# Layer norms of a transformer block moved from VectorE to ScalarE, with the routing and last scaling cut into short pieces and some TensorE pieces joined

## The reference, cut to what matters

```python
x = x + attention(layernorm(x))                  # 16 heads of 64, 4 key/value heads
x = x + cross_attention(layernorm(x), ctx, mask) # 16 heads of 16, 64 context rows per batch
z = layernorm(x)
# the feed-forward part, on every row z:
cluster = argmax(calibrate(z @ cluster_sigs.T))           # 8 clusters
tile    = argmax(calibrate(z @ sigs.T)[8 of the cluster]) # 8 tiles in each
comp    = tanh(gelu(z @ cw1 + cb1) @ cw2 + cb2)
mag     = relu(comp @ w1[tile] + b1[tile]) @ w2[tile] + b2[tile]
y       = z + mag * directions[tile] * output_scale
x = x + (y - mean(y)) / sqrt(var(y) + eps) * gamma + beta
```

## Time and profile before

| | us |
|---|---|
| three runs | 2066.41, 2067.19 (median), 2070.11 |
| the profiled execution, whole | 2067.07 |
| its span in the trace | 2065.3 |

### The profile page before, as it was taken

One profiled execution on the slowest core, in us unless ns is written; L12 is line 12 of the kernel. 1 busy time (PEld: TensorE's weight loads), 2 busy tenths in 40 slices (PEclk: granted clock), 3 DMA queues, 4 the chain that ended last, 5 costly groups with the idle time before them and its releaser, 6 DMA issues.

```text
span 2065.3 us, 27531 instructions
## 1 busy us (share of the span) xinstructions
PE 1855.6 (90%) x9556; PEld 912.9 (44%) x9556; DVE 1378.7 (67%) x2925; ACT 1135.1 (55%) x1507; POOL 979.1 (47%) x763
## 2 busy tenths in 40 slices
PE   3799999988999799998999988998899989998863
PEld 2444453443644344453554435444364434444342
DVE  4466756667576776756578585766657676677656
ACT  1367755655466554655456554665546654575422
POOL 2065545634554444652645345563465535463621
PEclk7799999999999999998999999999899999999895
DMA  4020000000200000010200000010010000000000
GB/s 150 1 62 1 1 1 1 12 21 1 62 11 1 1 21 1 1 32 0 62 11 1 1 0 21 1 32 0 11 41 1 1 0 21 1 1 1 21 0 10
DMA packets 22875, 32.01 MB, mean 15 GB/s; under 512 B 2577, under 2 KB 16977, under 8 KB 22737
## 3 DMA queue, kind: packets, MB, share of 16 engines
q1 hardware_dynamic: 22736, 30.26, 5.3%
HBM read 13.48 MB, written 4.19 MB: 9 GB/s over the span
## 4 chain that ended last, share of the span: by engine, by line
PE 70%; DVE 18%; issue 5%; ACT 4%; POOL 2%; DMA 0%; SPq 0%; POOLq 0%; DVEq 0%; ACTq 0%
PE attended L955 19%; PE key_scores L935 18%; PE misc L853 7%; PE misc L995 5%; PE max_scores L903 5%; DVE relu L1432 3%; PE misc L1019 3%; PE misc L965 2%; PE misc L921 2%; PE misc L1051 1%; PE misc L1010 1%; PE misc L1040 1%; PE misc L858 1%; DVE prob_sum L1446 1%; DVE buf_b L1328 1%
## 5 line engine op out<-in xcount | busy, mean ns | idle before, releaser
L1189 ACT ACTIVATE probs<-key_scores 128x1024 f32<-128x1024 f32 x512 | 524.5, 1024 | 602.1 <-PE key_scores L935 420.6
L1792 POOL TENSOR_TENSOR prob_sum<-prob_sum,probs 128x512 f32<-128x512 f32 x384 | 538.9, 1403 | 234.0 <-ACT probs L1189 212.8
L955 PE MATMUL attended<-probs,v_all 128*64 128x512 f32 x2048 | 577.1, 637 | 0.1
L1432 DVE CUSTOM_DVE_ANT_0 relu<-max_scores,relu 128x512 f32<-128x512 f32 x512 | 332.3, 686 | 263.7 <-PE max_scores L903 262.6
L935 PE MATMUL key_scores<-q_high,k_chain 64*128 64x512 f32 x2048 | 470.2, 455 | 10.7 <-ACT probs L1189 10.3
L935 PEld LDWEIGHTS key_scores<-q_high,k_chain 64*128 64x128 f32 x2048 | 197.4, 189 | 468.3 <-issue 251.5
L1446 DVE TENSOR_TENSOR prob_sum<-prob_sum,probs 128x512 f32<-128x512 f32 x384 | 375.6, 978 | 19.6 <-ACT probs L1189 8.9
L1173 ACT ACTIVATE relu<-max_scores 128x1024 f32<-128x1024 f32 x256 | 261.5, 1021 | 47.2 <-PE max_scores L903 47.2
L903 PE MATMUL max_scores<-k_max,q_high 64*128 64x512 f32 x1024 | 215.5, 416 | 75.4 <-DVE row_max L1432 73.9
L1788 POOL TENSOR_TENSOR prob_sum<-probs 128x512 f32<-128x512 f32 x64 | 87.8, 1371 | 345.6 <-PE misc L965 286.6
L935 PE MATMUL key_scores<-q_low,k_chain 64*128 64x512 f32 x1024 | 207.8, 402 | 0.0
(11 more groups left out here) (406 smaller groups left out, 2170.5 us busy)
## 6 DMA issues: line engine op xcount, KB each, us to landing
k_chain<-k_chain SPq DMA_DIRECT2D x32, 256.0 KB, 3.8
buf_a<-in_x SPq DMA_DIRECT2D x8, 512.0 KB, 4.9
k_max<-k_max SPq DMA_DIRECT2D x16, 256.0 KB, 3.7
x_in<-in_x SPq DMA_DIRECT2D x7, 512.0 KB, 4.2
out_x<-buf_b SPq DMA_DIRECT2D x7, 512.0 KB, 3.0
heads_out<-in_qkv_wT SPq DMA_DIRECT2D x1, 1536.0 KB, 8.5
wo<-in_o_wT SPq DMA_DIRECT2D x1, 1024.0 KB, 12.7
rows_sb<-in_rows SPq DMA_DIRECT2D x1, 646.0 KB, 10.4
```

What stands on the lines that cost most here:

```text
L955: tensor.matmul(attended[head * HD:(head + 1) * HD, :], v_all[:, kt, g * HD:(g + 1) * HD], prob_slot(u, kt, head), start=kt == 0, stop=kt ...
L1189: scalar.activation(probs[(u * KT + kt) % len(probs)][:, :, :], key_scores[:, :, :], ACT.Exp).then_inc(S["exp"])
L1432: vector.tensor_tensor_reduce(out=relu[:, head, :], in0=max_scores[:, head, :], in1=relu[:, head, :], scale=1.0, scalar=-3.4e38, op0=ALU.a ...
L1792: gpsimd.tensor_tensor(prob_sum[1][:, :], prob_sum[1][:, :], probabilities, ALU.add).then_inc(S["prob_sum1"])
```

## The change

It does the following:

- **Norms on ACT.** `x_norm` and `norm` leave DVE. ACT computes x * rstd + (-mean * rstd) with an Identity activation of 128x256 for each of the four tiles, scale and bias being columns of `rstd`. For that `rstd` on POOL has four instructions in place of two (add eps, -mean, power, product), each waiting for the one before.
- **Statistics behind the additions.** `bn_stats` follows each `x1`, `x2` and `y` directly (and each pair of tiles of x in the new piece `x_bn`); `stats` keeps only `bn_aggr`.
- **Short pieces.** `cal_b` and `cal_c` (6 and 7 instructions) become `cal_b` to `cal_f` (3, 3, 2, 2, 3) with a `yield LATE` between them; `first_max`, `pick_tiles` and `pick_one` get steps of their own; `spline` becomes `spline_a` and `spline_b` (4 and 4); `y`, `gamma`, `beta` go by pairs of tiles. No DVE instruction of these changes.
- **Joined pieces.** Both transposes of a norm stand in one step, so do both parts of `q2`, `route` with `compress`, and the `gathered` matmuls by two; `stats` moves to the step of the last `x1`, and an empty step behind the second norm is dropped.
- New waits protect the reused buffers (`ahead_of`: all signals that the plan gave before this entry).

The core of the diff (the cuts inside `cal_b` to `cal_f`, `spline_a` and `spline_b`, and the loops by pair in `y`, `gamma_` and `beta_` are as told above):

```diff
-    "x_stats": {"bn_stats": NT, "moments": NT, "var_eps": 1, "rstd": 1}, "x_norm": {"normed": NT},
+    "x_bn": {"bn_stats": 2}, "x_stats": {"moments": NT, "var_eps": 2, "rstd": 2}, "x_norm": {"normed": NT},
...
-    "out_proj": {"out_proj": 1}, "residual_bias": {"residual_bias": 1}, "x1": {"x1": 1},
-    "stats": {"bn_stats": NT_TIMES, "moments": NT_TIMES, "var_eps": 1, "rstd": 1}, "norm": {"normed": NT_TIMES},
+    "out_proj": {"out_proj": 1}, "residual_bias": {"residual_bias": 1}, "x1": {"x1": 1, "bn_stats": 1},
+    "stats": {"moments": NT_TIMES, "var_eps": 2, "rstd": 2}, "norm": {"normed": NT_TIMES},
...
+        self.so_far[entry] = dict(self.total)
...
 def x_prep(plan, t):
     yield LATE
+    plan.put("x_bn", t, 0)
+    yield LATE
+    plan.put("x_bn", t, 1)
     plan.put("x_stats", t)
     yield LATE
     plan.put("x_norm", t)
...
-    plan.put("cal_b", j, which)
-    yield LATE
-    plan.put("cal_c", j, which)
+    for part in "bcdef":
+        plan.put(f"cal_{part}", j, which)
+        if part != "f":
+            yield LATE
...
-        yield EARLY if i < nt - 1 else LATE
+        if i < nt - 1:
+            yield EARLY
     plan.put("stats", j, 1)
     yield LATE
     plan.put("norm", j, 1)
     yield EARLY
     for c in range(KC):
         plan.put_in_bank("norm_T", j, 1, c)
-        yield LATE
+    yield LATE
+    for c in range(KC):
         if c < nt // 2:
             plan.put("output_bias", j, c)
         plan.put("norm_ev", j, 1, c)
-        yield EARLY
+    yield EARLY
...
     for m in range(KC):
         plan.put_in_bank("q2", j, m)
-        yield LATE
+    yield LATE
+    for m in range(KC):
         plan.put("q2_ev", j, m)
-        yield EARLY
+    yield EARLY
...
     plan.put("norm", j, 2)
-    yield LATE
     yield EARLY
     for c in range(KC):
         plan.put_in_bank("norm_T", j, 2, c)
-        yield LATE
+    yield LATE
+    for c in range(KC):
         plan.put("norm_ev", j, 2, c)
-        yield EARLY
+    yield EARLY
     plan.put_in_bank("route", j)
+    plan.put_in_bank("compress", j)
     yield LATE
     plan.put("route_ev", j)
-    yield EARLY
-    plan.put_in_bank("compress", j)
-    yield LATE
     plan.put("gelu", j)
...
     plan.put("tanh_b", j)
     yield from clusters
+    yield LATE
     plan.put("first_max", j, 0)
+    yield LATE
     plan.put("pick_tiles", j)
-    yield LATE
     yield from calibration(plan, j, 1)
+    yield LATE
     plan.put("first_max", j, 1)
+    yield LATE
     plan.put("pick_one", j)
-    yield LATE
     yield EARLY
     plan.put_in_bank("pickT", j)
     yield LATE
     plan.put("pickT_ev", j)
     yield EARLY
-    for i in range(nt):
-        plan.put_in_bank("gathered", j, i)
+    for pair in range(nt // 2):
+        for i in range(2 * pair, 2 * pair + 2):
+            plan.put_in_bank("gathered", j, i)
         yield LATE
-        plan.put("gathered_ev", j, i)
-        yield EARLY if i < nt - 1 else LATE
-    plan.put("spline", j)
-    plan.put("y", j)
-    yield LATE
+        for i in range(2 * pair, 2 * pair + 2):
+            plan.put("gathered_ev", j, i)
+        if pair < nt // 2 - 1:
+            yield EARLY
+    yield LATE
+    plan.put("spline_a", j)
+    yield LATE
+    plan.put("spline_b", j)
+    for pair in range(nt // 2):
+        yield LATE
+        plan.put("y", j, pair)
     plan.put("stats", j, 3)
-    yield LATE
-    plan.put("gamma", j)
-    yield LATE
-    plan.put("beta", j)
     for pair in range(nt // 2):
+        yield LATE
+        plan.put("gamma", j, pair)
+    for pair in range(nt // 2):
+        yield LATE
+        plan.put("beta", j, pair)
         plan.put("x3", j, pair)
-        if pair < nt // 2 - 1:
-            yield LATE
     plan.put("store", j)
...
+        def ahead_of(signal, stage, *key):
+
+            return S[signal], plan.so_far[(stage, *key)].get(signal, 0)
...
+            def normalise(space, src, dst):
+                for i in range(space.nt):
+                    scalar.activation(dst[:, i, :], src[:, i, :], ACT.Identity, bias=space.rstd[:, 3, i:i + 1],
+                                      scale=space.rstd[:, 1, i:i + 1]).then_inc(S["normed"])
+
+            def x_norm(t):
+                act.wait_ge(*after("rstd", "x_stats", t))
+                normalise(main, x_of(t), x_of(t))
+
+            def norm(j, k):
+                act.wait_ge(*after("rstd", "stats", j, k))
+                if k == 1 and j:
+                    act.wait_ge(*after("store", "store", min(j, FIRST_HALF) - 1))
+                if k == 1 and j == 0:
+                    act.wait_ge(*after("v2", "v2", B - 1))
+                    act.wait_ge(*after("v2_block", "v2_block", B - 1))
+                    act.wait_ge(*after("mask_add", "mask"))
+                if k == 2:
+                    act.wait_ge(*after("norm_T", "norm_T", j, 1, KC - 1))
+                normalise(spaces[j], spaces[j].a, spaces[j].b)
...
-            def measure(space, src, stage, *key):
-                nt, base = space.nt, before("bn_stats", stage, *key)
-                for i in range(nt):
+            def bn_stats(space, src, tiles):
+                for i in tiles:
                     vector.bn_stats(space.stats[:, i, :], src[:, i, :]).then_inc(S["bn_stats"])
-                for i in range(nt):
-                    dve.wait_ge(S["bn_stats"], base + i + 1)
+
+            def moments(space, stage, *key):
+                dve.wait_ge(*ahead_of("rstd", stage, *key))
+                for i in range(space.nt):
                     vector.bn_aggr(space.moments[:, i, :], space.stats[:, i, :]).then_inc(S["moments"])
 
-            def normalise(space, src, dst):
-                for i in range(space.nt):
-                    vector.tensor_scalar(dst[:, i, :], src[:, i, :], space.moments[:, i, 0:1], space.rstd[:, 1, i:i + 1],
-                                         ALU.subtract, ALU.mult).then_inc(S["normed"])
+            def x_bn(t, pair):
+                dve.wait_ge(*x_loaded(t))
+                dve.wait_ge(*ahead_of("moments", "x_bn", t, pair))
+                bn_stats(main, x_of(t), range(2 * pair, 2 * pair + 2))
 
             def x_stats(t):
-                dve.wait_ge(*x_loaded(t))
-                dve.wait_ge(S["normed"], plan.counts.get(("normed", "x_norm", t), (0, 0))[0])
-                measure(main, x_of(t), "x_stats", t)
-
-            def x_norm(t):
-                dve.wait_ge(*after("rstd", "x_stats", t))
-                normalise(main, x_of(t), x_of(t))
+                dve.wait_ge(*after("bn_stats", "x_bn", t, 1))
+                moments(main, "x_stats", t)
...
+                dve.wait_ge(*after("x1", "x1", j, i))
+                dve.wait_ge(*ahead_of("moments", "x1", j, i))
+                bn_stats(spaces[j], buf_a, [i])
 
             def stats(j, k):
-                if k == 1:
-                    dve.wait_ge(*after("x1", "x1", j, tiles_of(j) - 1))
-                elif k == 2:
-                    dve.wait_ge(*after("x2", "x2", j, tiles_of(j) // 2 - 1))
-                else:
-                    dve.wait_ge(*after("y", "y", j))
-                measure(spaces[j], spaces[j].b if k == 3 else spaces[j].a, "stats", j, k)
-
-            def norm(j, k):
-                dve.wait_ge(*after("rstd", "stats", j, k))
-                if k == 1 and j:
-                    dve.wait_ge(*after("store", "store", min(j, FIRST_HALF) - 1))
-                normalise(spaces[j], spaces[j].a, spaces[j].b)
+                dve.wait_ge(*ahead_of("bn_stats", "stats", j, k))
+                dve.wait_ge(*ahead_of("gamma", "stats", j, k))
+                moments(spaces[j], "stats", j, k)
...
+                dve.wait_ge(*after("x2", "x2", j, pair))
+                dve.wait_ge(*ahead_of("moments", "x2", j, pair))
+                bn_stats(spaces[j], spaces[j].a, range(2 * pair, 2 * pair + 2))
...
             def rstd(space, stage, *key):
+                epsilons, roots = before("var_eps", stage, *key), before("rstd", stage, *key)
                 pool.wait_ge(*after("moments", stage, *key))
+                pool.wait_ge(*ahead_of("normed", stage, *key))
+                pool.wait_ge(*ahead_of("beta", stage, *key))
                 gpsimd.tensor_scalar(space.rstd[:, 0, :], space.moments[:, :, 1], EPS, None, ALU.add).then_inc(S["var_eps"])
+                pool.wait_ge(S["var_eps"], epsilons + 1)
+                gpsimd.tensor_scalar(space.rstd[:, 2, :], space.moments[:, :, 0], -1.0, None, ALU.mult).then_inc(S["var_eps"])
                 pool.wait_ge(*after("minus_half", "minus_half"))
-                pool.wait_ge(*after("var_eps", stage, *key))
+                pool.wait_ge(S["var_eps"], epsilons + 2)
                 gpsimd.tensor_tensor(space.rstd[:, 1, :], space.rstd[:, 0, :], minus_half[:, 0:space.nt],
                                      ALU.pow).then_inc(S["rstd"])
+                pool.wait_ge(S["rstd"], roots + 1)
+                gpsimd.tensor_tensor(space.rstd[:, 3, :], space.rstd[:, 2, :], space.rstd[:, 1, :],
```

(4 more changed lines are left out.)

124 lines of the change are left out of this document (72 added, 52 removed), and 2 rows, old and new, of the table SIGNALS.

## The result

The changed kernel took **2076.27 us** (median of 6 runs, 2073.76 to 2084.20), the kernel before in the same series 2068.89 (2066.41 to 2070.26). The ratio is **1.0044, 95% interval 1.0024 to 1.0063**: slower by 0.4%, where 1960 was forecast and 1920 to 2015 given as the range.

A forecast was written before the change was run, and what follows sets the result against it. PE was taken as the bound, losing 116 us idle and 60 to a slow clock. Idle -73, clock -40, prologue +3 and last tails +3 gave -107 from 2067.07: 1960 us, range 1920 to 2015.

The forecast's parts named there:

- What bounds the kernel: Main loop: PE is the bound, with 116 us idle and 60 us of slow clock, 176 us at most to win.
- room: Tails: each step leaves DVE 0.88 us free; steps times this, against routing and scaling work, with 3 us of lag allowed.
- Routing and scaling in short pieces: Main-loop tails: waits for row maxima and last routing instruction fall from 64.6 + 8.3 to 15 us, bounds 5 and 40.
- Statistics behind the additions: DVE: same instructions, 1.65 us for four, spread over steps where DVE waited for PE; cost 0.
- Joined pieces: Tails: no matmul or evacuation removed, two ACT evacuations in one step; cost 0, bounds 0 and 0.5 us each.
- Norms off DVE: Norms moved to ACT: 0.45 to 0.5 us each, 2.0 for four; 14 us of waits left, from 21.9 and some of 10.3.
- the slower rival: Main loop's 20 norms: ACT waits for POOL's rstd and holds exponentials and scores; 2091 us, chance 0.05.
- Clock: Main loop: PE's loss to the slow clock falls from 60 to 20 us as gaps shrink, -40.
- The ends: Prologue and last tails, outside the main loop: each forecast 3 us longer.
- prologue: Before the attention: chunk 1's x_T comes about 4 us later; +3 us, 0 to +5.
- Last tails: Serial chain at the end: about four statistics each 0.6 us later, plus ACT norms; +3 us, -3 to +6.
- DVE stays the bound: Rival, main loop: instructions in twice the steps are still late, each also waiting for POOL's sums; 2012 us, chance 0.14.

The follow-up runs named there:

- v_ends_pool1: v_ends with POOL's running sum of head 1 cut to one column from the third key tile on, that softmax left out: 1950.73 us.
- v_joins: The kernel before with statistics moved and pieces joined (with x_prep's extra step), norms on DVE, no cuts: 2106.68 us.
- v_ends_dve: v_ends with the layer norms back on DVE, cuts and joins kept: 2075.10 us.
- v_sum_all: v_ends with POOL's running sums of head 1 moved to DVE, whole output computed: 2011.45 us.
- v_ends: The changed kernel with old pieces in the last two half tails and x statistics in one piece for the first two batches: 2077.29 us.
- v_nocut: v_ends with routing and last scaling in the old long pieces, joins and ACT norms kept: 2097.11 us.
- v_norms: The kernel before with norms on ACT and statistics behind the additions, no cuts or joins: 2076.22 us.
- v_stats: The kernel before with only the statistics moved behind the additions: 2082.74 us.
- v_best: v_sum_all with the norms of the last chunk's two halves on DVE again: 2010.13 us.

## Why the prediction was wrong

**What bounds the kernel** was read rightly: 176 us of idling and slow clock, mostly behind DVE pieces. In v_ends_pool1 the idle time of the attention is 41 us, where the forecast had 43. That is no hit of its sum: those 41 were reached with POOL's sums taken away, which by itself brings the kernel before from 116 to 72.

**The step that failed is "room"**: steps times 0.88 us of DVE time, against work counted at the durations of the old places. That room was taken from a unit without a tail, where no short SBUF instruction stands beside POOL's sums; and the durations are no property of the instruction. What DVE spends in the attention above the shortest duration of each kind of instruction grew from 273 to 313 us, though 39 of the 273 had been the norms': some 79 us of new waiting, 65 of it in the tail's instructions on the tiles of routing and scaling (40 to 105) and 13 in the attention's own sums. (The expectations' 257 and 287 take somewhat longer durations as the quiet ones.) The forecast had seen the effect for the norm (1.05 against 0.48) and used it for the part that leaves DVE, not for the 40 instructions that were to be spread over twice the steps. The 15 us of row maxima and last routing waits were 66.0 (57.6 + 8.4).

**Routing and scaling in short pieces**: right in direction, far too large in size. Single stalls fell from 7.5 us (before) and 8.0 (v_joins) to 3.8. But from v_joins to v_ends_dve the waits for the row maxima and the last routing instruction fell from 92.8 (77.6 + 15.2) to 68.6 us (59.9 + 8.7), where the forecast took 72.9 to 15; in time the cuts win 29.7 us in a joined kernel, where 58 us of idling and most of 40 of the clock were put down to them.

**Statistics behind the additions**, put at 0, cost 13.9 alone. The work was the same but not "spread over steps in which DVE waited for PE": those of `y` joined a step that already had `spline` and four additions, and dividing that step, additions included, gave all of it back.

**Joined pieces**, put at 0 with 0.5 each as the bound, cost 23.6 with `x_prep`'s extra step. The forecast counted matmuls and evacuations and no order; at least 10 us are the new places of later pieces, up to 13 stay open.

**Norms off DVE**: one ACT instruction takes 0.59 us, not 0.45 to 0.5, but they overlap, and four are 2.07 us (4 x 29.0 / 56), as priced (2.0). What failed is the wait behind them: PE's waits for ACT's norm and for the exponential come to 27.6 us (10.1 + 17.5), with 6.5 for the norm's evacuation, where 14 was said. That is no less than the 32.2 (21.9 + 10.3) of before. The groups, busy us and mean ns:

```profile
L1146 ACT ACTIVATE buf_b<-buf_a,rstd 128x256 f32<-128x256 f32 x56 | 29.0, 596 | 0.8 <-POOL rstd L1821 0.8
...
L1146 ACT ACTIVATE x_in<-x_in,rstd 128x256 f32<-128x256 f32 x24 | 12.4, 589 | 1.7 <-POOL rstd L1821 1.6
```

The figure weighed there, 0.51 us by the Trainium skill, ScalarE: Activation LUTs, section Rules for kernel authors, is near the 0.52 of busy time for each (29.0 / 56). ACT's idle time ahead of the 80 norms of this stretch is 2.5 us, so the slower rival, ACT waiting for rstd, is out in the attention, although the sign was its own. It is not out behind it, as "The ends" shows.

**Clock**: 60 to 20 was forecast from idle time that did not fall; at 0.97 it stayed, and it rose to 0.99 only in versions without POOL's sums (cut or moved) and with less idling (79 us in v_sum_all's attention, 0.99; 112 in the changed one, 0.97).

**The ends**: prologue +3 forecast, 3.2 found. Last tails +3, bounds -3 to +6: 14.2 found in the profile. Two waits of PE's timeline there, for the norm of one half with the other half's work queued behind it, and ACT's norms that end them:

```profile
1974.23 0.66 PE L877 MATMUL key_scores<-consts_sb,weights 128*128 128x128 f32 x4 [4.17 <-ACT weights L1146]
...
1989.67 1.12 PE L877 MATMUL key_scores<-consts_sb,p2T 128*128 128x128 f32 x4 [3.60 <-ACT p2T L1146]
...
1973.09 1.09 ACT L1146 ACTIVATE weights<-weights,buf_c 128x256 f32<-128x256 f32 x2 [11.03 <-POOL buf_c L1821]
...
1988.53 1.09 ACT L1146 ACTIVATE p2T<-buf_c,probs 128x256 f32<-128x256 f32 x2 [6.25 <-POOL probs L1821]
```

ACT stands idle for 11.03 and 6.25 us there until POOL's last instruction of rstd: here, in the serial chain, its four instructions do lie on the path. By single profiles, so with some us of doubt each, the last stretch takes 4 to 5 us for the new pieces of the halves (126.8 to 122.2), 4 to 7 for ACT norms (v_ends 122.1 to v_ends_dve 116.5, v_nocut 115.7 to v_joins 108.8, v_norms 116.1 to v_stats 111.8; 3.1 by v_best), and 6 to 8 for the cuts in the tails before it (v_ends against v_nocut, v_ends_dve against v_joins). For the last a place can be seen: in v_ends_dve DVE still has `gamma` and `beta` of chunk 6 in the last 9 us of the attention, and the first addition of the halves begins 15.4 us behind the last exponential, in v_joins 8.5. They add up to more than 14.2, as other parts make the stretch shorter (v_joins has 108.8, the kernel before 112.6).

The rival **DVE stays the bound** had the mechanism ("each also waits for POOL's sums") at 0.14 and 2012 us. It was sized as half the gain lost; all of it was, so its 2012 missed as well.

## What to carry to other kernels

Before cutting DVE work into pieces, sort its instructions by what they read. Here additions with two SBUF inputs, and `tensor_scalar` from SBUF to SBUF, often lasted until the GpSimd instruction beside them ended (1057 ns against 328, 588 against 168), so many tiny dependent ones are a poor thing to spread beside a stream of GpSimd sums. Try moving the sums first: here 448 GpSimd additions of 1.26 to 1.78 us became 0.78 us each on DVE, the kernel before 1.4% faster and the changed one 2.7%. And an edit that "only moves" work has a price: here 13.9 and 23.6 us. Ask what else is in the step that it is moved to.

## What the runs showed of the hardware

A DVE instruction on 8 columns took 1.24 us beside a GpSimd addition of 1.64, and 168 ns on average in v_ends_pool1. Row maxima from PSUM (687 and 688 ns), statistics (423) and the reduction of 224 columns (386) were the same in the changed kernel and in v_ends_pool1, which has little of GpSimd's sums. GpSimd's sums vary as well: 1.26 us at best, and 1.64 in the window shown; that DVE is the reason is not shown. And two kernels with the same output can differ in their scatter: six runs of v_ends spread over 15.8 us, four of v_sum_all over 1.3.
